# Two graph attention layers on one core: all stages of layer 0 before all of layer 1, adjacency loaded for every stage, one regular order

## The chip, the core and the metric

The kernel runs on one core of a Trainium2 chip. The metric is the device time of one execution in microseconds. The engines named here are PE (TensorE), DVE (VectorE), ACT (ScalarE), POOL (GpSimd) and SP (SyncE), which in this kernel only issues DMAs.

## The reference

Two layers act on x (8 batches, 1024 nodes, 128 features, float32) with a 0/1 adjacency adj (8, 1024, 1024, int32):

```
def _L0_gnn_ref(h, adj, W, a):
    Wh = jnp.einsum('bni,io->bno', h, W)
    e1 = Wh @ a1
    e2 = Wh @ a2
    e = e1[:, :, None] + e2[:, None, :]
    e = jnp.where(e > 0, e, ALPHA * e)
    scores = jnp.where(adj > 0, e, neg)
    attention = jax.nn.softmax(scores, axis=2)
    h_prime = jnp.einsum('bnm,bmo->bno', attention, Wh)
    return jax.nn.elu(h_prime)
...
h = jnp.maximum(_layernorm(x, axis=-1), 0.0)
x = x + _L0_gnn_ref(h, adj, L0_gnn_W, L0_gnn_a)
h = jnp.maximum(_layernorm(x, axis=-1), 0.0)
x = x + _L1_gnn_ref(h, adj, L1_gnn_W, L1_gnn_a)
```

Layer 1 is the same attention with other weights and without the elu. Both layers use the same adjacency of a batch.

## The kernel before, in words

The work is cut into 16 stages, one for each pair of layer and batch; `stages[n]` is that pair. The order before is layer 0 of batches 0, 1 and 2, then alternately layer 1 of batch b and layer 0 of batch b + 3, then layer 1 of batches 5, 6 and 7. The adjacency of a batch stays in one of three slots of `adj_sb` from its layer 0 to its layer 1, so each batch's adjacency (eight tiles of 128 x 1024) is loaded once.

The five engines have programs of their own, written out by hand, and meet through semaphores. In iteration n of its loop each engine finishes stage n - 1, runs stage n and prepares stages n + 1 and n + 2:

- PE: `project(n + 1)` makes W h of the next stage and the two attention terms from `hT`; `attend(n, t)` multiplies the masked weights of tile t (`pbuf`) into eight accumulators (`acc`); `spread_emax` and `turn_r` are single transposes; `transposes(n + 2)` turns the normalised x of a later stage. `spread_r` is eight transposes in the place of `turn_r`: it brings the row of exponentials to all partitions through PSUM.
- DVE: `masks(n, t)` makes `pbuf` from the row, a column and the adjacency tile; `take_acc(n - 1)` copies the three accumulator banks (`accs`) and takes the reciprocal; `copy_e` and `exp_args` prepare the exponentials of stage n + 1; `statistics` and `moments` are the layernorm statistics of a later stage; `add_elu` and `add_x` (after a layer 0 stage) or `add_hp` (after a layer 1 stage) update x.
- ACT: `scale_accs`, `exps`, `copy_r` (the row for the DMA) or `copy_row` (the spread row), `elu_exp`, `normalise`, `scale_wh`, `copy_hT`.
- POOL: the power for the layernorm.
- SP: all DMAs but four, in the order of its program. `load_row(m)` waits for `rT_ready`, writes the row to DRAM, waits for that, and reads it back broadcast to 128 partitions. An issue behind a wait in SP's program comes no earlier than that wait.

The DVE's masks of stage n + 1, t = 0, need `row_in` (or `row_copied`) and that PE is past the first tiles of stage n. PE's first product of stage n needs `acc_copied`, that is the copy of the accumulators of stage n - 1 by DVE. `before_drain(n)` is how many masks of stage n DVE makes before that copy.

Two stages (`LATE`, stages 3 and 15 here) need x of a stage only three places earlier, and the engines take other orders around them; stage n = 1 and stage n = AHEAD - 1 = 2 have orders of their own too. Stages in `SPREAD` (1 and 15) get their row by `spread_r`, the others by `load_row`. Stage n starts for PE where its `project(n + 1)` starts (in the regular order).

Of the kernel before, what the change touches and what calls it, by code (L numbers as in the profile page):

```python
# [5 lines left out]
P = 128  # L6
F32 = mybir.dt.float32
I32 = mybir.dt.int32
# [10 lines left out]
def gat_two_layers(nc, x, adj, w0, w0t, a0, w1, w1t, a1, r_rows, out):  # L19
# [7 lines left out]
    AHEAD = 3  # L27
    X_SLOTS = 6
# [15 lines left out]
    LATE = tuple(stage_of[1, b] for b in range(B) if stage_of[1, b] - stage_of[0, b] == 3)  # L44


    SPREAD = (1, LAST)
# [8 lines left out]
    with ExitStack() as ctx:  # L56
# [17 lines left out]
        adj_sb = sb("adj_sb", [P, AHEAD * T * N], I32)  # L74
        x_sb = sb("x_sb", [P, X_SLOTS * T * D])
# [40 lines left out]
        adj_in = [[sem(f"adj_in{s}_{t}") for t in range(T)] for s in range(AHEAD)]  # L116
# [60 lines left out]
        def x_at(b):  # L177
            s = (b % X_SLOTS) * T * D
            return x_sb[:, s:s + T * D]
# [4 lines left out]
        def adj_at(b, t):  # L184
            s = ((b % AHEAD) * T + t) * N
# [21 lines left out]
        def _(sp):  # L207
            def load_x(b):
                if b >= X_SLOTS:
                    sp.wait_ge(out_stored[b - X_SLOTS], 16)  # L210
                sp.dma_start(x_at(b), xv[b]).then_inc(x_in[b], 16)

            def load_adj(b, t):
                if b >= AHEAD:
                    sp.wait_ge(p_ready, T * stage_of[1, b - AHEAD] + t + 1)
                sp.dma_start(adj_at(b, t), adj[b, t]).then_inc(adj_in[b % AHEAD][t], 16)
# [29 lines left out]
            load_row(2)  # L246
            load_x(4)
            load_x(5)
            load_row(AHEAD)

            for n in range(AHEAD, LAST):
                l, b = stages[n]
                loads = l == 1 and b + AHEAD < B
                l_old, b_old = stages[n - 3]
                if l_old == 1 and b_old + X_SLOTS < B:
                    load_x(b_old + X_SLOTS)
# [77 lines left out]
        def _(act):  # L334
# [137 lines left out]
            for n in range(1, LAST + 1):  # L472
                elu = stages[n - 1][0] == 0
                if n == AHEAD - 1:

                    scale_accs(n - 1)
                    copy_hT(n + 1)
                    elu_exp(n - 1)
                    normalise(n + 2)
                    exps(n + 1)  # L480
                    copy_r(n + 1)
                    scale_wh(n + 1)
                    copy_hT(n + 2)
                    continue
                if n + 1 in LATE:
                    copy_hT(n + 1)
# [3 lines left out]
                if n + 2 in LATE:  # L490
                    elu_exp(n - 1)
                if n < LAST:
                    exps(n + 1)
                    if n + 1 in SPREAD:
                        copy_row(n + 1)
                    else:
                        copy_r(n + 1)
                    if n + 2 not in LATE:
                        elu_exp(n - 1) if elu else None
                    if n + 2 <= LAST and n + 2 not in LATE:  # L500
                        normalise(n + 2)
                    scale_wh(n + 1)
                if n + 2 in LATE:
                    normalise(n + 2)
                elif n + 2 <= LAST:
                    copy_hT(n + 2)

        @block.vector
        def _(dve):
# [145 lines left out]
            def masks(n, tiles):  # L655
                l, b = stages[n]
                for t in tiles:
                    if l == 0:
                        dve.wait_ge(adj_in[b % AHEAD][t], 16 * (b // AHEAD + 1))
                    if n == 0:  # L660
                        dve.wait_ge(row0_ready, 2)
                    elif t == 0:
# [3 lines left out]
                        else:  # L666
                            dve.wait_ge(row_in, 16 * loaded_rows(n))
                    nc.vector.scalar_tensor_tensor(pbuf[:, t, :], row_r[:, n % 2, :],  # L668
                                                   sqr[:, n % 2, 0, t:t + 1], adj_at(b, t),
# [83 lines left out]
            for n in range(1, LAST):  # L753
                l, b = stages[n - 1]
                if n + 2 <= LAST and not {n + 1, n + 2} & set(LATE):
                    statistics(n + 2)
                    moments(n + 2)
                masks(n, range(before_drain(n)))
                take_acc(n - 1)
                if n + 1 in LATE:  # L760
                    masks(n, (2, 3))
                    if n + 2 <= LAST:
                        statistics(n + 2)
                        moments(n + 2)
                    masks(n, (4,))
                    copy_e(n + 1)
                    masks(n, (5,))
                    exp_args(n + 1)
                elif n == 1:
                    copy_e(n + 1)  # L770
                    masks(n, (4,))
                    exp_args(n + 1)
                    masks(n, (5,))
                    add_elu(b)
                    add_x(b)
                    masks(n, (6,))
                    statistics(n + 2)
                    moments(n + 2)
                    masks(n, (7,))
                    continue  # L780
                elif n + 2 in LATE:
                    masks(n, (3,))
                    copy_e(n + 1)
                    masks(n, (4,))
                    exp_args(n + 1)
                    masks(n, (5,))
                    add_elu(b)
                    add_x(b)
                    statistics(n + 2)
                    moments(n + 2)  # L790
                    masks(n, (6, 7))
                    continue
                else:
                    if before_drain(n) == 1:
                        masks(n, (1,))
                    copy_e(n + 1)
                    masks(n, (2,))
                    exp_args(n + 1)
                    masks(n, (3, 4, 5))
# [16 lines left out]
        def _(pe):  # L816
# [176 lines left out]
            for n in range(1, LAST):  # L993
                if n + 1 in LATE:
                    k = 1 if n + 1 in SPREAD else 2
                    attend(n, range(k))
                    transposes(n + 1)
                    attend(n, (k,))
                    project(n + 1)
                    attend(n, (k + 1,))  # L1000
                    spread_emax(n + 1)
                    attend(n, (k + 2,))
                    spread_r(n + 1) if n + 1 in SPREAD else turn_r(n + 1)
                    attend(n, range(k + 3, 6))
                else:
                    project(n + 1)
                    attend(n, (0,))
                    spread_emax(n + 1)
                    attend(n, (1, 2) if n + 2 in LATE else (1,))
                    turn_r(n + 1)  # L1010
                    attend(n, (3, 4, 5) if n + 2 in LATE else (2, 3, 4, 5))
# [36 lines left out]
```

## Time and profile before

| what | value |
|---|---|
| time, median of 3 runs | 298.88 us (298.63 to 299.03) |
| the profiled execution: its own time | 298.75 us |
| its span in the trace | 296.9 us |
| PE, DVE, ACT, POOL busy | 290.6, 268.1, 167.3, 48.5 us |
| DMA moved | 49.50 MB, 167 GB/s mean |

The span runs from the first to the last instruction of the trace; the execution's own time has 1.85 us around it. Busy times are sums over one engine; matmul ends are modelled.

### The profile page before, as it was taken

To read this page: it belongs to the slowest core of one execution; us is meant where nothing else is said; L and a number is where in the kernel's file an instruction comes from. 1 tells how busy PE (TensorE), PEld (TensorE's weight loads), DVE (VectorE), ACT (ScalarE), POOL (GpSimd) and SP (SyncE) were. 2 spreads that over 40 slices of the span, in tenths; PEclk is the share of its full clock that TensorE was granted. 3 is DMA by queue.
4 is the path that set the end of the run, shared out by engine and by line. 5 is a ranking of instruction groups with operands and counts; after the bars stand their busy time and mean duration, and the time that the engine had idled before them with its cause. 6 is when DMAs were issued, how large, how long until landed. Compare 5 with 4: busy or idle time off the path is not lost.

```text
span 296.9 us, 6592 instructions
## 1 busy us (share of the span) xinstructions
PE 290.6 (98%) x2562; PEld 287.8 (97%) x2562; DVE 268.1 (90%) x613; ACT 167.3 (56%) x490; POOL 48.5 (16%) x53
## 2 busy tenths in 40 slices
PE   7999999999999999999999999999999999999996
PEld 7889999999999999999999999999999999999996
DVE  4796899889999989999899989999899989988796
ACT  3377482983856539382683737566393836384310
POOL 2712003205021120303003030210303000400000
PEclk9999999999999999999999999999999999999999
DMA  7999935004690347714584344903566110101012
GB/s 238 416 408 406 407 148 212 2 7 138 195 371 3 143 153 252 305 33 164 161 305 192 144 128 142 367 8 141 149 227 265 68 77 0 73 0 72 1 73 71
DMA packets 15215, 49.50 MB, mean 167 GB/s; under 512 B 2024, under 2 KB 3280, under 8 KB 15184
## 3 DMA queue, kind: packets, MB, share of 16 engines
q1 hardware_dynamic: 14608, 48.69, 44.4%
q8 instruction: 20, 0.33, 0.4%
q10 hardware_dynamic: 576, 0.39, 0.4%
q14 instruction: 11, 0.09, 0.1%
HBM read 44.83 MB, written 4.25 MB: 165 GB/s over the span
## 4 chain that ended last, share of the span: by engine, by line
PE 86%; DVE 7%; issue 2%; DMA 2%; ACT 2%; POOL 1%; DVEq 0%; POOLq 0%; ACTq 0%
PE acc L950 64%; PE prj L888 8%; PE tp L827 4%; DVE pbuf L668 3%; PE acc L965 2%; PE acc L819 2%; DMA row_r<-r_rows 1%; ACT xn L376 1%; DVE stats L563 1%; PE prj L891 1%; POOL rstd L281 1%; PE prj L860 1%; PE tp L910 1%; DVE accs L677 1%; PE prj L965 1%
## 5 line engine op out<-in xcount | busy, mean ns | idle before, releaser
L950 PE MATMUL acc<-wh,pbuf 128*128 128x129 f32 x1968 | 229.6, 275 | 0.9 <-DVE pbuf L644 0.3
L950 PEld LDWEIGHTS acc<-wh,pbuf 128*128 128x128 f32 x1968 | 225.1, 192 | 1.6 <-issue 0.9
L668 DVE SCALAR_TENSOR_TENSOR pbuf<-row_r,sqr,adj_sb 128x1024 f32<-128x1024 f32 x127 | 157.5, 1276 | 1.4 <-ACT row_r L416 1.0
L281 POOL TENSOR_TENSOR rstd<-vareps,neg_half 128x8 f32<-128x8 f32 x15 | 38.5, 2568 | 202.3 <-DVE vareps L581 202.2
L426 ACT ACTIVATE accs<-accs,rec 128x128 f32<-128x128 f32 x120 | 36.7, 389 | 51.0 <-DVE rec L687 51.0
L376 ACT ACTIVATE xn<-x_sb,shift,rstd 128x128 f32<-128x128 f32 x120 | 47.6, 478 | 0.0
L396 ACT ACTIVATE wh<-prj,wh 128x128 f32<-128x128 f32 x120 | 31.9, 357 | 0.0
L888 PE MATMUL prj<-w_ext,hT 128*128 128x130 f32 x240 | 29.3, 275 | 0.0
L888 PEld LDWEIGHTS prj<-w_ext,hT 128*128 128x128 f32 x240 | 28.0, 191 | 0.0
L382 ACT ACTIVATE hT<-tp 128x1024 f32<-128x1024 f32 x15 | 15.4, 1024 | 20.3 <-PE tp L827 20.3
L677 DVE TENSOR_TENSOR accs<-acc,uniform 128x387 f32<-128x387 f32 (+1 forms) x45 | 20.5, 506 | 2.9 <-PE acc L950 2.8
L563 DVE BATCH_NORM_STATS2 stats<-x_sb 128x6 f32<-128x128 f32 x112 | 22.9, 275 | 0.0
L827 PE MATMUL tp<-ident,xn 128*128 128x128 f32 x128 | 17.4, 277 | 0.3 <-DVE pbuf L668 0.3
L827 PEld LDWEIGHTS tp<-ident,xn 128*128 128x128 f32 x128 | 14.7, 142 | 1.0 <-DVE pbuf L668 0.4
L606 DVE COPY ecol<-prj 128x12 f32<-128x12 f32 x15 | 2.5, 167 | 10.8 <-PE prj L891 10.8
L373 ACT ACTIVATE act_gate<-shift 128x1 f32<-128x1 f32 x15 | 2.9, 192 | 14.1 <-POOL shift L284 14.1
L387 ACT ACTIVATE sqr<-args 128x24 f32<-128x24 f32 x15 | 3.3, 219 | 11.8 <-DVE args L640 11.8
L698 DVE TENSOR_TENSOR x_sb<-x_sb,ex 128x1024 f32<-128x1024 f32 x8 | 9.7, 1217 | 0.1
L692 DVE SCALAR_TENSOR_TENSOR ex<-accs,ex 128x1024 f32<-128x1024 f32 x8 | 9.7, 1218 | 0.0
L438 ACT ACTIVATE ex<-ex 128x1024 f32<-128x1024 f32 x8 | 8.5, 1058 | 0.3
L704 DVE TENSOR_TENSOR x_sb<-accs,x_sb 128x1024 f32<-128x1024 f32 x7 | 8.5, 1218 | 0.0
L436 ACT ACTIVATE ex<-accs 128x1024 f32<-128x1024 f32 x8 | 8.4, 1046 | 0.1
(105 smaller groups left out, 155.6 us busy)
## 6 DMA issues: line engine op xcount, KB each, us to landing
adj_sb<-in_adj SPq DMA_DIRECT2D x64, 512.0 KB, 6.5
row_r<-r_rows SPq DMA_DIRECT2D x13, 512.0 KB, 4.2
x_sb<-in_x SPq DMA_DIRECT2D x7, 512.0 KB, 6.4
out_x<-x_sb SPq DMA_DIRECT2D x7, 512.0 KB, 3.0
x_sb<-in_x ACTq DMA_DIRECT2D x1, 256.0 KB, 3.6
x_sb<-in_x SPq DMA_DIRECT2D x1, 256.0 KB, 3.4
r_rows<-rT SPq DMA_DIRECT2D x13, 4.0 KB
out_x<-x_sb SPq DMA_DIRECT2D x1, 192.0 KB, 1.9
```

Source lines behind the costliest of these rows:

```text
L281: nc.gpsimd.tensor_tensor(rstd[:, :], vareps[:, :], neg_half[:, :], ALU.pow).then_inc(rstd_ready, 1)
L376: nc.scalar.activation(xn[:, t, :], src[:, t, :], ACT.Identity, bias=shift[:, t:t + 1], scale=rstd[:, t:t + 1]).then_inc(xn_ready, 1)
L382: nc.scalar.activation(hT[:, :], tp[:, :], ACT.Relu, accum_out=hsum[:, :]).then_inc(hT_ready, 1)
L396: nc.scalar.activation(wh[:, m % 2, t, 0:D], prj[:, k, s * E:s * E + D], ACT.Copy, scale=wh[:, m % 2, t, D:C]).then_inc(wh_ready, 1)
L426: op = nc.scalar.activation(hp[:, t, :], hp[:, t, :], ACT.Copy, scale=rec[:, t:t + 1])
L563: st = nc.vector.bn_stats(stats[:, t, :], src[:, t, :])
L668: nc.vector.scalar_tensor_tensor(pbuf[:, t, :], row_r[:, n % 2, :], sqr[:, n % 2, 0, t:t + 1], adj_at(b, t), ALU.max, ALU.min).then_inc(p_ ...
L677: nc.vector.tensor_tensor(accs[:, k * NB:k * NB + w, :], acc[:, k, 0:w * C].rearrange("p (s c) -> p s c", c=C), uniform[:, e % 2, :].unsqu ...
L692: nc.vector.scalar_tensor_tensor(ex[:, :, :], hp, 0.0, ex[:, :, :], ALU.max, ALU.subtract).then_inc(hp_free, 1)
L827: return nc.tensor.transpose(tp[:, t * P:(t + 1) * P], xn[:, t, :], ident[:, :])
L888: nc.tensor.matmul(prj[:, k, s * E:(s + 1) * E], hT[:, t * P:(t + 1) * P], w_ext[:, l, :], start=(s == 0), stop=True, skip_group_check=True)
L950: mm = nc.tensor.matmul(sum_at(k, s), pbuf[:, t, i * P:(i + 1) * P], wh[:, n % 2, t, :], start=(t == 0 and s == 0 and k < NB), stop=(t == ...
```

## The change

The stages now run all of layer 0 (batches 0 to 7), then all of layer 1. The adjacency no longer stays for a second use: `load_adj(n, t)` takes a stage, not a batch, loads for every one of the 16 stages, and reuses slot n mod 3 when the masks of stage n - 3 have read the tile. `x_sb` holds all eight batches, so loading x waits for no store. Every distance between the layers of a batch is eight stages, and the orders of their own go: stages 1 to 14 follow one order on PE, DVE and ACT. Only stage 1 keeps `spread_r` and its four masks before the copy; stage 15 gets its row by `load_row`.

```
-    stages = [(0, b) for b in range(AHEAD)]
-    for b in range(B - AHEAD):
-        stages += [(1, b), (0, b + AHEAD)]
-    stages += [(1, b) for b in range(B - AHEAD, B)]
+    stages = [(l, b) for l in range(2) for b in range(B)]
...
-    SPREAD = (1, LAST)
+    SPREAD = (1,)
...
-            return {1: 4, AHEAD: 1, LAST - 2: 3}.get(n, 2)
+            return 4 if n == 1 else 2
...
             def load_x(b):
-                if b >= X_SLOTS:
-                    sp.wait_ge(out_stored[b - X_SLOTS], 16)
                 sp.dma_start(x_at(b), xv[b]).then_inc(x_in[b], 16)
...
+            def load_adj(n, t):
+                if n >= ADJ_SLOTS:
+                    sp.wait_ge(p_ready, T * (n - ADJ_SLOTS) + t + 1)
+                sp.dma_start(adj_at(n, t), adj[stages[n][1], t]).then_inc(adj_in[n % ADJ_SLOTS][t], 16)
...
-            load_row(2)
-            load_x(4)
-            load_x(5)
-            load_row(AHEAD)
...
+            for n in range(1, LAST):
+                loads = n + 2 <= LAST
                 if loads:
                     for t in range(3):
-                        load_adj(b + AHEAD, t)
-                if n + 1 not in SPREAD:
-                    load_row(n + 1)
+                        load_adj(n + 2, t)
+                load_row(n + 1)
+                if n + 3 < B:
+                    load_x(n + 3)
                 if loads:
                     for t in range(3, T):
-                        load_adj(b + AHEAD, t)
+                        load_adj(n + 2, t)
...
             for n in range(1, LAST):
                 l, b = stages[n - 1]
-                if n + 2 <= LAST and not {n + 1, n + 2} & set(LATE):
+                if n + 2 <= LAST:
                     statistics(n + 2)
                     moments(n + 2)
-                masks(n, range(before_drain(n)))
+                k = before_drain(n)
+                masks(n, range(k))
                 take_acc(n - 1)
...
-                elif n == 1:
-                    copy_e(n + 1)
-                    masks(n, (4,))
-                    exp_args(n + 1)
-                    masks(n, (5,))
-                    add_elu(b)
-                    add_x(b)
-                    masks(n, (6,))
-                    statistics(n + 2)
-                    moments(n + 2)
-                    masks(n, (7,))
-                    continue
...
+                copy_e(n + 1)
+                masks(n, (k,))
+                exp_args(n + 1)
+                masks(n, range(k + 1, 6))
...
             for n in range(1, LAST):
...
+                project(n + 1)
+                attend(n, (0,))
+                spread_emax(n + 1)
+                attend(n, (1,))
+                turn_r(n + 1)
+                attend(n, (2, 3, 4, 5))
+                if n + 2 <= LAST:
                     transposes(n + 2)
                 attend(n, (6, 7))
```

On DVE, from the last two masks of stage 0 to the copy of its accumulators, the kernel before runs (`pbuf` is a mask, `accs` an accumulator copy):

```order
L668 SCALAR_TENSOR_TENSOR pbuf<-row_r,sqr,adj_sb 128x1024 x6
L677 TENSOR_TENSOR accs<-acc,uniform 128x387 x2
L677 TENSOR_TENSOR accs<-acc,uniform 128x258
L687 RECIPROCAL rec<-accs 128x8
L606 COPY ecol<-prj 128x12
```

The changed kernel runs at the same place:

```order
L629 SCALAR_TENSOR_TENSOR pbuf<-row_r,sqr,adj_sb 128x1024 x2
L523 MEMSET gate 128x1
L526 BN_STATS stats<-x_sb 128x6 x8
L532 TENSOR_TENSOR mdiff<-stats 128x8
L534 SCALAR_TENSOR_TENSOR m2sum<-stats 128x8
L536 TENSOR_TENSOR mean<-stats 128x8
L539 SCALAR_TENSOR_TENSOR between<-mdiff 128x8
L541 TENSOR_SCALAR negmean<-mean 128x8
L544 SCALAR_TENSOR_TENSOR vareps<-m2sum,between 128x8
L629 SCALAR_TENSOR_TENSOR pbuf<-row_r,sqr,adj_sb 128x1024 x4
L638 TENSOR_TENSOR accs<-acc,uniform 128x387 x2
L638 TENSOR_TENSOR accs<-acc,uniform 128x258
```

The statistics and moments of stage 3 have moved in between the masks of stage 0 and those of stage 1.

On SP, from the end of the initial loads to the third row, the kernel before issues (`adj_sb<-in_adj` is an adjacency tile, `r_rows<-rT` and `row_r<-r_rows` the two halves of `load_row`):

```order
L216 DMA adj_sb<-in_adj 128x1024 x8
L221 DMA r_rows<-rT 8x128
L223 DMA row_r<-r_rows 128x1024
L211 DMA x_sb<-in_x 128x1024 x2
L221 DMA r_rows<-rT 8x128
L223 DMA row_r<-r_rows 128x1024
L216 DMA adj_sb<-in_adj 128x1024 x3
```

The changed kernel issues there:

```order
L207 DMA adj_sb<-in_adj 128x1024 x11
L212 DMA r_rows<-rT 8x128
L214 DMA row_r<-r_rows 128x1024
L202 DMA x_sb<-in_x 128x1024
L207 DMA adj_sb<-in_adj 128x1024 x8
L212 DMA r_rows<-rT 8x128
L214 DMA row_r<-r_rows 128x1024
L202 DMA x_sb<-in_x 128x1024
L207 DMA adj_sb<-in_adj 128x1024 x8
```

Three tiles of stage 3 now stand ahead of the first row, and one x and eight tiles between two rows.

On PE, in the last but one stage, the kernel before ends its preparation of stage 15 with:

```order
L896 MATMUL tp<-ident,emax 128x128
L950 MATMUL acc<-wh,pbuf 128x129 x8
L910 MATMUL tp<-ident,sqr 128x128 x8
L950 MATMUL acc<-wh,pbuf 128x129 x38
```

The changed kernel has there:

```order
L822 MATMUL tp<-ident,emax 128x128
L876 MATMUL acc<-wh,pbuf 128x129 x8
L844 MATMUL tp<-ident,sqr 8x128
L876 MATMUL acc<-wh,pbuf 128x129 x54
```

The eight transposes of `spread_r` have become the single one of `turn_r`.

## Rows read from the trace of the kernel before

**Rows 1.** The page: busy time, and 40 slices of 7.42 us each.

```profile
PE 290.6 (98%) x2562; PEld 287.8 (97%) x2562; DVE 268.1 (90%) x613; ACT 167.3 (56%) x490; POOL 48.5 (16%) x53
...
PEclk9999999999999999999999999999999999999999
...
GB/s 238 416 408 406 407 148 212 2 7 138 195 371 3 143 153 252 305 33 164 161 305 192 144 128 142 367 8 141 149 227 265 68 77 0 73 0 72 1 73 71
```

**Rows 2.** Windows by stage: busy time of each engine, clock, DMA share, GB/s.

```profile
34.79:51.52 16.73, 16.52 (x148) 16.33 (x148) 15.28 (x38) 8.76 (x26) 2.81 (x2) 1.00 0.54 217
51.52:88.49 36.97, 36.45 (x322) 35.88 (x323) 34.72 (x90) 25.61 (x71) 8.03 (x5) 1.00 0.39 139
88.49:105.89 17.40, 17.40 (x159) 17.38 (x158) 17.19 (x40) 9.45 (x30) 4.21 (x4) 1.00 0.23 82
105.89:123.29 17.40, 17.40 (x158) 17.38 (x158) 16.04 (x37) 11.48 (x32) 1.86 (x2) 1.00 0.76 268
```

**Rows 3.** The chain that ended last, in order of time: start, us, what.

```profile
36.80 1.79 PE acc L950 x16
...
42.27 0.12 PE tp L918
...
42.71 1.21 DMA r_rows<-rT
43.94 4.35 DMA row_r<-r_rows
...
271.81 0.87 PE tp L910 x8
```

**Rows 4.** Timeline of DVE, 12 to 90 us: start, us, what, idle before.

```profile
29.68 4.87 DVE L668 SCALAR_TENSOR_TENSOR pbuf<-row_r,sqr,adj_sb 128x1024 f32<-128x1024 f32 x4 [1.03 <-ACT row_r L416]
34.47 1.35 DVE L677 TENSOR_TENSOR accs<-acc,uniform 128x387 f32<-128x387 f32 x3
...
48.42 2.48 DVE L668 SCALAR_TENSOR_TENSOR pbuf<-row_r,sqr,adj_sb 128x1024 f32<-128x1024 f32 x2 [0.37 <-DMA row_r<-r_rows]
50.83 1.35 DVE L677 TENSOR_TENSOR accs<-acc,uniform 128x387 f32<-128x387 f32 x3
...
73.69 0.16 DVE L606 COPY ecol<-prj 128x12 f32<-128x12 f32 x1
```

**Rows 5.** Timeline of SP's queue: the load of x of batch 3.

```profile
15.04 1.07 SPq L211 DMA_DIRECT2D x_sb<-in_x  x1
```

**Rows 6.** DMA issues in 15.0 to 15.1 us: KB, us to landing.

```profile
x_sb<-in_x SPq DMA_DIRECT2D x1, 512.0 KB, 15.9
```

**Rows 7.** Timeline of DVE, 88 to 124 us.

```profile
89.32 1.35 DVE L677 TENSOR_TENSOR accs<-acc,uniform 128x387 f32<-128x387 f32 x3
...
90.83 0.12 DVE L606 COPY ecol<-prj 128x12 f32<-128x12 f32 x1
...
107.94 0.17 DVE L606 COPY ecol<-prj 128x12 f32<-128x12 f32 x1 [1.08 <-PE prj L891]
...
114.23 1.22 DVE L692 SCALAR_TENSOR_TENSOR ex<-accs,ex 128x1024 f32<-128x1024 f32 x1
...
118.90 0.29 DVE L563 BATCH_NORM_STATS2 stats<-x_sb 128x6 f32<-128x128 f32 x1
...
123.74 0.55 DVE L677 TENSOR_TENSOR accs<-acc,uniform 128x387 f32<-128x387 f32 x1
```

**Rows 8.** Timeline of ACT, 105 to 124 us.

```profile
110.77 0.22 ACT L387 ACTIVATE sqr<-args 128x24 f32<-128x24 f32 x1 [1.43 <-DVE args L640]
...
112.97 1.06 ACT L438 ACTIVATE ex<-ex 128x1024 f32<-128x1024 f32 x1
```

**Rows 9.** DMA issues near 44.3, 119.4 and 148.7 us: KB, us to landing.

```profile
x_sb<-in_x SPq DMA_DIRECT2D x1, 512.0 KB, 5.2
...
x_sb<-in_x SPq DMA_DIRECT2D x1, 512.0 KB, 7.3
...
adj_sb<-in_adj SPq DMA_DIRECT2D x1, 512.0 KB, 5.4
```

More of the change, by code:

```diff
@@ L26, in gat_two_layers @@
     HALF = T // 2
-    AHEAD = 3
-    X_SLOTS = 6
+    ADJ_SLOTS = 3
     LAST = 2 * B - 1
@@ L115, in gat_two_layers @@
         x_in = [sem(f"x_in{b}") for b in range(B)]
-        adj_in = [[sem(f"adj_in{s}_{t}") for t in range(T)] for s in range(AHEAD)]
+        adj_in = [[sem(f"adj_in{s}_{t}") for t in range(T)] for s in range(ADJ_SLOTS)]
         out_stored = [sem(f"out_stored{b}") for b in range(B)]
@@ L489, in _ @@
                 scale_accs(n - 1)
-                if n + 2 in LATE:
-                    elu_exp(n - 1)
                 if n < LAST:
                     exps(n + 1)
[L494 to L500, printed above, removed]
+                    copy_r(n + 1)
+                    elu_exp(n - 1) if elu else None
+                    if n + 2 <= LAST:
                         normalise(n + 2)
                     scale_wh(n + 1)
-                if n + 2 in LATE:
-                    normalise(n + 2)
-                elif n + 2 <= LAST:
+                if n + 2 <= LAST:
                     copy_hT(n + 2)
@@ L655, in masks @@
             def masks(n, tiles):
-                l, b = stages[n]
                 for t in tiles:
-                    if l == 0:
-                        dve.wait_ge(adj_in[b % AHEAD][t], 16 * (b // AHEAD + 1))
+                    dve.wait_ge(adj_in[n % ADJ_SLOTS][t], 16 * (n // ADJ_SLOTS + 1))
                     if n == 0:
@@ L754, in _ @@
                 l, b = stages[n - 1]
-                if n + 2 <= LAST and not {n + 1, n + 2} & set(LATE):
+                if n + 2 <= LAST:
                     statistics(n + 2)
                     moments(n + 2)
-                masks(n, range(before_drain(n)))
+                k = before_drain(n)
+                masks(n, range(k))
                 take_acc(n - 1)
-                if n + 1 in LATE:
-                    masks(n, (2, 3))
-                    if n + 2 <= LAST:
-                        statistics(n + 2)
-                        moments(n + 2)
-                    masks(n, (4,))
-                    copy_e(n + 1)
-                    masks(n, (5,))
-                    exp_args(n + 1)
-                elif n == 1:
[L770 to L773, printed above, removed]
-                    add_elu(b)
-                    add_x(b)
-                    masks(n, (6,))
-                    statistics(n + 2)
-                    moments(n + 2)
-                    masks(n, (7,))
[L780 to L799, printed above, removed]
+                copy_e(n + 1)
+                masks(n, (k,))
+                exp_args(n + 1)
+                masks(n, range(k + 1, 6))
                 if l == 0:
@@ L993, in _ @@
             for n in range(1, LAST):
[L994 to L1011, printed above, removed]
-                if n + 2 <= LAST and n + 2 not in LATE:
+                project(n + 1)
[4 more added lines that the diff above has]
+                attend(n, (2, 3, 4, 5))
+                if n + 2 <= LAST:
                     transposes(n + 2)
```

34 lines of the change are left out of this document (6 added, 28 removed).

## The prediction, made before the changed kernel was run

> **What bounds the kernel now.** I read the page first, then the windows by stage, then the chain that ended last, and only then the single engines around the first four stages. The page [rows 1] says PE 98% busy, with the granted clock at its upper level (2.4 GHz) in all 40 slices. The windows [rows 2] say where the missing 2% lies. A regular stage (project, eight attend tiles, two small transposes, eight transposes of a later stage) takes exactly 17.40 us, with PE busy for 17.40 of them, whether the DMA share is 0.76 or 0.23. So from 88.49 us on, the kernel is PE's own work, and nothing gained on DVE, ACT or DMA is worth anything there; DMA traffic doesn't slow PE either. Before that, stage 1 takes 16.73 us although it holds no transposes (17.40 less the 0.87 of eight transposes [rows 3], so 16.53), and stages 2 and 3 take 36.97 us where their content is 2 x 17.40 + 0.87 = 35.67. The whole slack outside start and tail is thus 0.20 + 1.30 = 1.50 us.
>
> **The change, part by part.** The sum is made against the profiled execution: span 296.9 us, its own time 298.75, that is 0.13 below the median of 298.88.
>
> 1. The last stage's row. PE's eight spreading transposes (0.87 us in the chain) become one transpose (0.12, as in the other stages) [rows 3]. PE is the bound there, so -0.75. The row now comes by DMA: turn to write 0.44, write to broadcast 1.23, landing 4.35, together 6.02 us after a transpose at 5.7 us into stage 14, so it lands near 11.7; the masks of stage 15 were reached no earlier than that in a regular stage (from the statistics' end at 13.0 + 2.4 us on), and PE asks for them only at its stage end, 16.5. Hidden.
>
> 2. The irregular orders of stages 1 to 3 go. If the regular order runs there as it does later, all 1.50 us of slack come back: -1.50.
>
> 3. A wait is put in the place of them. The regular order puts the statistics of stage n+2 ahead of the masks of stage n, in n = 1 too. There they are those of batch 3, and SP still loads batch 3's x behind sixteen adjacency tiles. It is issued at 15.04 [rows 5] and lands 15.9 later [rows 6], at 30.94. In the kernel before, DVE ends the masks of stage 0 at 28.65, idles 1.03 for the row and starts stage 1's masks at 29.68 [rows 4]; x of batch 3 is asked for only after all of these. Now DVE waits for it: start at 31.07 (a mask started 0.13 after its row landed, 43.94 + 4.35 = 48.29 against 48.42 [rows 3, 4]), statistics 2.44 (118.90 to 123.74 is 4.84, less two masks of 1.20 [rows 7]), four masks 4.79 (29.68 to 34.47), so the accumulators are copied from 38.30 instead of 34.47. Behind the waiting statistics on DVE stand the masks of stage 1 and this copy, and for the copy waits PE: its first product of the next stage came 0.69 after a copy began (50.83 [rows 4]; the window boundary 51.52 [rows 2] is that product). So PE goes on at 38.99, where it was ready at 36.80 [rows 3]: +2.19. Nothing hides it: PE has no other work between, since the transposes of stage 3 stand later.
>
> 4. What is late next. Stage 2 begins at 34.79 + 17.40 + 2.19 = 54.38. On DVE: copy_e 1.51 after the copies begin (89.32 to 90.83 [rows 7]), at 39.81; the exponentials start 2.83 and end 3.05 after copy_e (107.94 [rows 7]; 110.77 + 0.22 [rows 8]), at 42.9 at most, and PE reaches its transpose at 38.99 + 1.79 + 0.12 + 1.79 = 42.7. The row write is issued 0.44 later, at 43.2 to 43.3. Three more adjacency tiles now lie in the queue ahead of it: SP's run of tiles without a row has eleven instead of eight, as the order shows. The initial loads fill the queue at 408 GB/s until about 39.7 (slice six, from 37.1, holds 148 GB/s [rows 1]); three tiles of 0.524 MB add 3.9 us, to 43.6, and their landing about 45.0. The write lands between 44.5 (no hindrance, 1.23) and 45.0. x of batch 4 is now issued right behind the row, 0.39 later (43.94 to 44.33), and lands 5.2 to 5.4 after its issue: 5.2 is x in this very place, 5.4 an adjacency tile of the same size in this place with more tiles behind [rows 9]. So x lands at 50.1 to 50.8. DVE arrives there at about 50.2: it also waits for ACT's elu, done 3.26 after the exponentials start (110.77 to 112.97 + 1.06 [rows 8], 0.5 of it a wait that is shorter here), so at 42.64 + 2.8 to 3.3, near 45.5; from the add of the elu to the statistics it is 4.67 (114.23 to 118.90 [rows 7]). Copies for stage 1 then begin at 55.1 to 55.8, 0.7 to 1.4 into stage 2, where a regular stage has 0.45. PE needs the first bank at 2.01 - 0.69 = 1.32, and its row transpose has 0.59 to spare. That is 0 to 0.4 us of stall; I take 0.15, nearer the lower end, because DVE's uninterrupted cycle (73.69 to 90.83, 17.14 us, with all of the elu work in it [rows 4, 7]) regains 0.26 per stage.
>
> 5. The regular loop with x in it. x of stages 4 to 7 is now fetched one stage ahead, right behind the row, where before it had stages of room. This makes a closed loop: copy_e to exponentials 3.05, turn to write 0.44, write to row issue 1.23, to x issue 0.39, landing 5.4, 0.13, statistics and two masks 4.84, copies to copy_e 1.51: 16.99 us, against PE's 17.40. It costs nothing as long as x lands within 5.8 us of its issue. Bounds: 0 at 5.4; for 7.3 see the rivals.
> The Trainium skill speaks against this place: "DMA: Bandwidth & Descriptors", section "Latency and other measured facts", gives HBM's latency as 0.2 us on average and 2 us at high load. By an estimate from that page, 1.8 us more would put the landing at 7.2 and the loop at 18.8. The trace doesn't bear it out at this spot: the same landing is 5.2 in an idle queue and 5.4 with four tiles following.
>
> 6. Twice the adjacency traffic: 8 x 0.524 + x 0.524 + row 0.524 = 5.2 MB, 12.8 us at 408 GB/s of each 17.40. Issued from 7.3 us into a stage, it is through 4.3 us into the next, before the next row write at 6.1. Cost 0; it was already so in the stage with share 0.76 [rows 2]. The cover is 1.8 us; gone, it would feed the loop of point 5. Larger x storage drops SP's waits for stores: no one waited there, 0.
>
> Sum: -0.75 - 1.50 + 2.19 + 0.15 = +0.09. Span 297.0, time 298.84 for the profiled run, 298.97 beside the median: I say **299.0**. A difference under 0.2%, 0.6 us, is about what a measurement of this kernel can't tell from none. Own range of this case: stall of point 4 from 0 to 0.9 and landing of x of batch 3 within half a microsecond: 298.3 to 300.2.
>
> **The rivals.**
> A, slower: the x loop of point 5 binds. Decides at a landing of 5.8 us. For it: a late x took 7.3 [rows 9], though behind five adjacency tiles, and the loop has only 0.41 us. Against: in its new place it has none ahead. At 6.4, midway between these ends, the loop is 17.99, 0.59 too long, four times, less the 0.59 in hand: +1.8, 300.8. At 7.3: 4 x 1.49 - 0.59 = +5.4, 304.4. Chance 0.17.
> B, faster: the wait for batch 3 isn't paid, as x lands by 29 or PE's order absorbs it. Then 2.19 and 0.15 fall away: 296.7. Against: the landing row [rows 6], and SP's order up to there, which the change leaves alone. Chance 0.10.
> C, slower: DVE becomes the bound in the eight stages in a row that carry elu work; before, a lighter one followed each. 17.14 against 17.40 says no, but only 0.26 is left. If hand-overs between engines make it 17.7, eight stages cost 0.3 each: 301.4. Chance 0.08.
> D, slower: the 2.2 us gap lowers PE's clock to 1.2 GHz. The 1.50 us of gaps in stages 1 to 3, spread over three stages, did not [rows 1, 2]. If a fifth of stage 1's remaining 15.4 us ran at half speed, +3.1: 302. Chance 0.04.
> The Trainium skill, "TensorE: Matmul & The Clock Gate", section "HAM oscillation", says that idle gaps let the gate fall back; no gap of this trace is long enough to show it.
> Something unlisted: 0.03.
>
> **How the numbers follow.** My case has 0.58, so 299.0 is the prediction. Outside 297.6 to 302.0 lie B (0.10), the dear half of A (0.08) and little else. Faster by over 0.2%: B and 0.09 of my case, 0.19. Within: 0.41. Slower: A, C, D, the rest of my case and the unlisted, 0.40.
>
> **What would show it.** Step 3: DVE idle about 2.4 us before the first statistics of stage 1's iteration, released by DMA x, and PE idle near 2.2 us at 36.8, released by the accumulator copy. Step 1: stage 14 of 16.53 us, no spreading transposes. Step 2: stages 2 and 3 of 17.40 each with a little on top. Step 5: x landing 5.2 to 5.8 after its issue, and DVE no later into stages 3 to 6 than 1.1 us at its copies. I am wrong if stages 2 to 6 exceed 17.6, if the clock shows under 1.0 after 39 us, or if PE doesn't wait at 36.8.

## The result and the profile after

| | before | changed |
|---|---|---|
| median of 12 executions | 298.88 us | 301.7 us |
| lowest | 298.50 us | 298.85 us |
| the profiled execution, its own time | 298.75 us | 299.89 us |
| its span | 296.9 us | 298.1 us |
| DMA moved | 49.50 MB | 83.59 MB |

The ratio of changed to before is 1.0063, 95% interval 1.004 to 1.0086: slower by 0.6%. It is close to the ratio of the means (301.04 to 299.21 us); the medians alone are 0.9% apart, because the changed kernel's median falls into the dearer of two groups. These groups differ in the granted clock: four executions at 1.00 took 298.85 to 299.99 us, seven at 0.994 or 0.989 took 301.26 to 302.52 us. The twelfth, 374.26 us at a clock of 0.85, was disturbed and is left out of what follows. The profiled execution belongs to the first group.

The page of the changed kernel, to be held against [rows 1] (busy time, 40 slices of 7.45 us, DMA traffic):

```profile
PE 289.7 (97%) x2555; PEld 287.2 (96%) x2555; DVE 268.2 (90%) x613; ACT 166.4 (56%) x489; POOL 47.8 (16%) x53
...
PE   7999969999999999999999999999999999999996
...
GB/s 230 417 405 409 407 353 226 403 200 411 191 365 329 247 411 153 412 125 308 327 247 385 112 411 138 346 342 220 374 214 401 209 320 382 208 291 118 25 73 70
```

PE has one hole, in the sixth slice, where before it had none. The windows by stage of the changed kernel (boundaries near those of its stages, columns as in [rows 2]: PE busy, PE weight loads, DVE, ACT, POOL, granted clock, DMA share, GB/s):

```profile
34.79:54.30 19.51, 16.78 (x151) 16.62 (x150) 16.49 (x39) 11.47 (x32) 3.08 (x2) 1.00 0.83 314
54.30:71.70 17.40, 17.34 (x156) 17.18 (x155) 17.20 (x40) 11.47 (x32) 3.02 (x3) 1.00 0.81 320
71.70:89.10 17.40, 17.40 (x158) 17.38 (x158) 17.08 (x39) 11.47 (x32) 2.95 (x3) 1.00 0.75 299
```

The first row lacks 2.7 us of PE, the second next to nothing, the third is full: DVE has 17.1 us of work in each 17.40 and PE doesn't wait for it, at twice the adjacency traffic. The two timelines around the hole, DVE's and PE's, answer to [rows 4] and [rows 3]:

```profile
26.35 2.48 DVE L629 SCALAR_TENSOR_TENSOR pbuf<-row_r,sqr,adj_sb 128x1024 f32<-128x1024 f32 x2
31.77 0.29 DVE L526 BATCH_NORM_STATS2 stats<-x_sb 128x6 f32<-128x128 f32 x1 [2.94 <-issue]
...
34.22 4.87 DVE L629 SCALAR_TENSOR_TENSOR pbuf<-row_r,sqr,adj_sb 128x1024 f32<-128x1024 f32 x4
39.01 1.35 DVE L638 TENSOR_TENSOR accs<-acc,uniform 128x387 f32<-128x387 f32 x3
```

```profile
36.59 0.39 PE L817 MATMUL prj<-w_ext,hsum 128*128 128x128 f32 x2
39.71 2.02 PE L876 MATMUL acc<-wh,pbuf 128*128 128x129 f32 x16 [2.73 <-DVE accs L638]
```

And the load of x of batch 3, in the timeline of SP's queue and with its time to landing:

```profile
15.15 1.07 SPq L202 DMA_DIRECT2D x_sb<-in_x  x1
```

```profile
x_sb<-in_x SPq DMA_DIRECT2D x1, 512.0 KB, 16.6
```

15.15 + 16.6 = 31.75, and DVE starts its statistics at 31.77. The view puts that wait down as "issue", since it names no DMA there; the landing time names it. PE waits 2.73 us for the accumulator copy at the end of that queue of work. In this execution the clock stays at 1.00 throughout; no execution of the changed kernel with a low clock was profiled.

### The profile page after: what moved, and what is told of

The parts are those of the page before. It is cut to its first block, busy times and chain, and to the rows that moved or that the text cites. A ratio compares the mean times of both kernels' runs of the same rounds, so it can differ in the third digit from the quotient of the medians.

```text
span 298.1 us, 6643 instructions
## 1 busy us (share of the span) xinstructions
PE 289.7 (97%) x2555; PEld 287.2 (96%) x2555; DVE 268.2 (90%) x613; ACT 166.4 (56%) x489; POOL 47.8 (16%) x53
## 2 busy tenths in 40 slices
DMA packets 24591, 83.59 MB, mean 280 GB/s; under 512 B 3072, under 2 KB 4336, under 8 KB 24560
## 4 chain that ended last, share of the span: by engine, by line
PE 92%; DVE 5%; issue 2%; POOL 0%; ACT 0%; POOLq 0%; DVEq 0%
PE acc L876 70%; PE prj L814 8%; PE tp L753 5%; DVE pbuf L629 3%; PE acc L891 2%; PE acc L745 2%; PE prj L817 1%; PE prj L786 1%; PE tp L822 1%; PE prj L891 1%; PE prj L876 1%; PE acc L795 1%; PE tp L844 1%; DVE stats L526 0%; PE tp L828 0%
## 5 line engine op out<-in xcount | busy, mean ns | idle before, releaser
L405 ACT ACTIVATE rT<-tp 8x128 f32<-8x128 f32 x14 | 3.7, 267 | 6.2 <-PE tp L844 6.2
```

## The experiments

Each ratio is to executions of the kernel before that ran beside the run. "Low clock" counts the executions with a granted clock under 0.998. Of the 69 undisturbed executions of the kernel before beside these runs, one had a low clock (304.82 us at 0.989). Twelve of the 28 beside e1 to e4 took 299.87 to 300.59 us with the clock at 1.00, about 1.5 us more than the others; why stays open, and those four ratios hold that spread.

| run | median us | ratio to before (95%) | low clock | PE gap in the profiled execution |
|---|---|---|---|---|
| changed kernel | 301.7 | 1.0063 (1.004 to 1.0086) | 7 of 11 | 2.73 at 37 us |
| e1_x3_early | 299.84 | 1.0015 (0.999 to 1.0041) | 5 of 12 | 2.91 at 54, 0.41 at 75 us |
| e2_gap_filled | 299.67 | 1.0012 (0.9995 to 1.0029) | 0 of 12 | filled |
| e3_gap_in_before | 303.45 | 1.0152 (1.0119 to 1.0185) | 5 of 6 | 2.17 at 37, 0.49 at 55 us |
| e4_traffic_in_before | 299.18 | 0.9993 (0.9973 to 1.0012) | 0 of 12 | as before |
| e5_x3_x4_early | 297.89 | 0.9967 (0.9949 to 0.9984) | 0 of 12 | 0.63 at 54, 1.66 at 72 us |
| e6_x3_x4_row2_early | 297.66 | 0.9962 (0.9939 to 0.9985) | 1 of 12 | 1.06 at 72 us |
| e7_last_row_only | 303.67 | 1.0155 (1.0126 to 1.0184) | 6 of 6 | 3.64 at 279 us |
| e8_after_again | 300.62 | 1.0054 (1.0026 to 1.0082) | 6 of 12 | 2.12 at 37, 0.18 at 74 us |
| e9_x_one_stage_ahead | 296.77 | 0.9934 (0.9908 to 0.9959) | 0 of 6 | none |
| e10_row15_spread | 297.24 | 0.9943 (0.9923 to 0.9962) | 0 of 6 | none |
| e11_x_behind_tiles | 334.96 | 1.1205 (1.1155 to 1.1255) | 6 of 6 | 2.76, 6.86, 6.76, 5.84, 6.88 |

### Is it the wait for x of batch 3? (e1)

```
+            load_x(3)
             for t in range(T):
                 load_adj(1, t)
-            load_x(3)
```

> The changed kernel with one line moved: x of batch 3 is loaded ahead of stage 1's adjacency tiles instead of behind them. Theory (the wait for x of batch 3 on DVE holds PE up, and the gap in PE is what lowers the granted clock in some executions): DVE starts stage 3's statistics near 28.9 us without a wait, PE's gap at 36.8 falls from 2.7 us to under 0.3, the span falls by 2.7 to 2.9 us to 295.2 to 295.5, the time to about 297.1, and the granted clock stays 1.00 in every execution, so the spread of the times closes to under 0.5 us. Rival (the constant adjacency traffic, 280 GB/s, is behind the slower executions): the span still falls by 2.7 us at best, but executions with a clock of 0.994 and 2 to 3 us more go on appearing in about half of the runs.

The hole at 37 us went, as both theories said, but the time hardly fell, as neither did. Five of twelve executions still had a low clock, as the rival said; whether the new hole or the traffic is behind them, this run can't tell. PE's and DVE's timelines of this kernel show it one stage later:

```profile
53.60 0.39 PE L817 MATMUL prj<-w_ext,hsum 128*128 128x128 f32 x2
56.90 2.02 PE L876 MATMUL acc<-wh,pbuf 128*128 128x129 f32 x16 [2.91 <-DVE accs L638]
```

```profile
51.35 0.29 DVE L526 BATCH_NORM_STATS2 stats<-x_sb 128x6 f32<-128x128 f32 x1 [3.85 <-issue]
```

This wait is for x of batch 4. The SP queue of this kernel shows why:

```profile
40.71 0.34 SPq L212 DMA_DIRECT2D r_rows<-rT  x1
45.33 0.35 SPq L214 DMA_DIRECT2D row_r<-r_rows  x1
45.72 0.43 SPq L202 DMA_DIRECT2D x_sb<-in_x  x1
```

The row's write of 4 KB, 1.2 us in an empty queue [rows 3], took 4.6, because the eleven tiles issued before it were still running: the DMA share is 1.02 up to 43 us, 0.58 in 43 to 44 and 0.19 in 44 to 45. The row and x came behind it. In the changed kernel the shares of 43 to 45 us are the same (0.57, 0.18), but its write is issued only at 44.07. So x of batch 4 lands at nearly the same time in both, 51.3 here (45.72 + 5.6) and 51.8 there (46.37 + 5.4): the backlog of the initial loads sets it, and a PE that is 2.7 us earlier waits for it that much longer. My expectation missed this.

### Traffic or gap: what lowers the clock? (e2, e3, e4, e8)

e2 fills PE's gap with work that computes nothing, and leaves the wait:

```
                 project(n + 1)
+                if n == 1:
+                    for _ in range(24):
+                        nc.tensor.transpose(tp[:, 0:P], ident[:, :], ident[:, :])
                 attend(n, (0,))
```

> The changed kernel with 24 transposes of the identity into the idle transpose tile, placed where PE waits for the accumulator copy (about 2.6 us of PE work that computes nothing). The wait for x stays. Theory (gap lowers the clock): the time of an execution with the clock at 1.00 is unchanged, about 299.1 to 299.9, give or take 0.3, but no execution shows a clock under 0.998, and the median falls from 301.7 to about 299.5. Rival (traffic, or the kernel's power, lowers the clock): executions at 0.994 and 301 to 302.5 us remain as frequent.

No execution of 12 had a low clock, and the median fell to 299.67. The traffic is that of the changed kernel.

e3 puts the gap alone into the kernel before; the extra statistics go to a scratch tile and change no result:

```
+                if n == 1:
+                    dve.wait_ge(x_in[3], 16)
+                    for t in range(12):
+                        nc.vector.bn_stats(scratch[:, t, :], x3_at(3)[:, t % T, :])
                 masks(n, range(before_drain(n)))
```

> The kernel before with the stall alone: ahead of stage 1's masks DVE waits for x of batch 3 and does twelve statistics of 128x128 into a scratch tile (2.45 us, the length of the changed kernel's statistics and moments). Traffic and order stay as before. Theory: DVE starts at about 31.1, PE gets a gap of 2.0 to 2.9 us at 36.8, the time rises by 2 to 3 us, and if the gap lowers the clock some executions show 0.994 and 2 to 3 us more on top. Rival (traffic): the gap costs its own length and no execution shows a lower clock than the kernel before does.

Its profiled execution is one with a low clock. PE's timeline and the windows (PE busy, PE weight loads, DVE, ACT, POOL, granted clock, DMA share, GB/s):

```profile
38.94 3.12 PE L955 MATMUL acc<-wh,pbuf 128*128 128x129 f32 x16 [2.17 <-DVE accs L678]
41.85 0.42 PE L901 MATMUL tp<-ident,emax 128*128 128x128 f32 x1
42.07 4.22 PE L955 MATMUL acc<-wh,pbuf 128*128 128x129 f32 x32
```

```profile
36.00:39.00 3.00, 0.83 (x8) 0.67 (x7) 3.00 (x4) 0.00 (x0) 0.00 (x0) 1.00 1.03 414
39.00:42.00 3.00, 3.00 (x17) 3.00 (x18) 2.46 (x8) 2.13 (x8) 0.00 (x0) 0.61 0.24 96
42.00:45.00 3.00, 3.00 (x24) 3.00 (x23) 2.53 (x7) 2.76 (x6) 0.00 (x0) 0.82 0.00 0
45.00:48.00 3.00, 3.00 (x29) 2.98 (x28) 2.96 (x3) 1.57 (x7) 0.00 (x0) 1.00 0.03 7
```

The clock is at its upper level while PE idles, falls once PE works again, and is back before 45 us. In windows of half a microsecond it is 1.00 up to 39.5, 0.50 (the lower level, 1.2 GHz) in each from 40 to 43, and 1.00 again from 43.5. In 39 to 45 us PE is busy throughout and gets through 41 matmul records (17 + 24), where 6 us at 1.00 hold 58 (two such windows as the last, of 29). The dear parts are the first tile, 3.12 us instead of 2.02, and the next two, 4.22 instead of 3.74. With the 0.15 of the small transpose that is 1.7 us. At this moment the DMA share was 0.24 and then 0. So a gap alone does it, without the added traffic. The span is 4.4 us above that of the kernel before (301.3 to 296.9). The gap of 2.17, a second one of 0.49 at 55.3 us behind a late row, and the clock's 1.7 make 4.36. The one execution of six with the clock at 1.00 took 303.49 us, so in this kernel the clock's price is not visible between executions. Something besides the clock differs between them, perhaps the gaps; that wasn't looked at.

e4 puts the traffic alone into the kernel before: the adjacency is loaded for each stage, in the old order of stages. Its core:

```
-            def load_adj(b, t):
-                if b >= AHEAD:
-                    sp.wait_ge(p_ready, T * stage_of[1, b - AHEAD] + t + 1)
-                sp.dma_start(adj_at(b, t), adj[b, t]).then_inc(adj_in[b % AHEAD][t], 16)
+            def load_adj(n, t):
+                if n >= AHEAD:
+                    sp.wait_ge(p_ready, T * (n - AHEAD) + t + 1)
+                sp.dma_start(adj_at(n, t), adj[stages[n][1], t]).then_inc(adj_in[n % AHEAD][t], 16)
```

> The kernel before in its own stage order, with its adjacency loaded for every stage (twice the traffic, slots by stage). Theory: traffic is hidden, the time is within 0.3 us of the kernel before, 298.9, with a clock of 1.00. Rival (traffic slows PE or lowers the clock): 1 to 3 us more, or executions with 0.994 in about half of the runs.

299.18 us, ratio 0.9993, clock 1.00 in all 12. A window over eight stages of it shows PE filling all of its time under a DMA share of 0.76:

```profile
123.29:263.00 139.71, 139.71 (x1253) 139.37 (x1252) 132.96 (x291) 82.51 (x246) 21.75 (x16) 1.00 0.76 291
```

e8 repeats the changed kernel as it is.

> The changed kernel once more, on the chip and between the runs of this call. Theory: two groups of times again, about 299 to 300 us with the clock at 1.00 and 301 to 302.5 us with 0.994, the second in about half of the executions. Rival (the groups belong to the chip of the first runs): one group only.

Six executions at 1.00 took 298.8 to 300.03 us; six at 0.988 to 0.994 took 301.21 to 304.17. The groups belong to the kernel. The profiled execution, one at 1.00, has x of batch 3 landed earlier than the first time (statistics from 31.21 instead of 31.77) and a gap of 2.12 instead of 2.73 us: the gap's length varies between executions. Together these four runs show that the gap lowers the clock and the traffic doesn't: filled, it goes (0 of 12); put in alone, it comes (5 of 6); the traffic alone does nothing (0 of 12).

### Removing the gaps (e5, e6, e9)

e5 also loads x of batch 4 early, ahead of stage 2's tiles.

> The changed kernel with x of batch 3 loaded ahead of stage 1's adjacency tiles and x of batch 4 ahead of stage 2's (it stood behind row 2). Theory (with x of batch 3 early the same gap only moved: DVE then waited 3.85 us for x of batch 4, which stood behind row 2 and its eleven tiles, and PE got its 2.9 us gap at 54 us): both gaps go; what stays is row 2 itself, issued near 46.6 and landing near 50.9, about when DVE wants it, so at most 0.3 us of gap at 54. Span 295.0 to 295.4, time about 297.0, clock 1.00 in every execution. Rival (a fixed backlog: whatever loads first, some transfer is late by 2.5 us around 50 us): the gap at 54 stays at 2 us or more and the time stays above 298.5.

```
+            load_x(3)
             for t in range(T):
                 load_adj(1, t)
-            load_x(3)
+            load_x(4)
...
-                if n + 3 < B:
+                if n > 1 and n + 3 < B:
                     load_x(n + 3)
```

The first kernel faster than before. But 0.63 us of gap stay at 54 (DVE waits 1.59 for row 2), and 1.66 at 72 us (DVE waits 2.12 for x of batch 5). The profiled execution is the slowest of the twelve (299.05 us), so the typical gaps may be smaller. My figure of 297.0 was 0.9 low, again for the backlog one stage further on; its rival had it half right.

e6 issues row 2 ahead of stage 3's tiles as well:

```
-                if loads:
+                if loads and n > 1:
                     for t in range(3):
                         load_adj(n + 2, t)
                 load_row(n + 1)
+                if n == 1:
+                    for t in range(3):
+                        load_adj(n + 2, t)
```

> As the one before, and in iteration 1 SP issues row 2 ahead of the three tiles of stage 3 instead of behind them. Theory: row 2 lands near 46.5, DVE waits for nothing in stages 1 and 2, PE has no gap over 0.1 us from 35 us on; span 294.9, time 296.7, clock 1.00 in every execution: 2.2 us under the kernel before (0.75 of the last row, 1.50 of the slack). Rival (DVE is too slow for eight elu stages in a row): a gap in PE appears in stages 3 to 8 and eats the gain.

The gap at 54 is gone, the one at 72 stays at 1.06. The SP queue of this kernel tells where x of batch 5 loses its time: the write of row 3 takes over 3 us.

```profile
58.12 0.29 SPq L212 DMA_DIRECT2D r_rows<-rT  x1
61.36 0.33 SPq L214 DMA_DIRECT2D row_r<-r_rows  x1
61.73 0.43 SPq L202 DMA_DIRECT2D x_sb<-in_x  x1
```

Nothing waits for DVE in stages 4 to 8, so the rival (DVE too slow for eight such stages) is out.

e9 keeps what e6 has (x of batches 3 and 4 and row 2 early) and gives every later x a stage more too: behind row n + 1 comes x of batch n + 4. The line that differs, against the changed kernel:

```
-                if n + 3 < B:
-                    load_x(n + 3)
+                if n + 4 < B:
+                    load_x(n + 4)
```

> The changed kernel with every x loaded one stage earlier: x of batches 3 and 4 ahead of stage 1's and stage 2's tiles, x of batch n + 4 behind row n + 1, and row 2 ahead of stage 3's tiles. Theory (what is left of the loss after the last experiment is one more x behind a row whose write stands in the backlog of tiles: DVE waited 1.84 us for x of batch 5 and PE 1.06 us at 72): that gap goes too; row 3 lands near 66.8, just before DVE wants it near 67.5. No PE gap over 0.3 us after 30 us, span 294.6 to 294.9, time 296.4 to 296.8 in every execution with the clock at 1.00; the spread of 3 us between executions, which comes from landing times, shrinks to under 1 us. Rival (the backlog moves the wait on to row 3): DVE waits 1 us or more for row 3 near 67.5, and PE has about 0.5 to 1 us at 72.

Windows of stages 1 and 2 of this kernel, and the count from its page:

```profile
34.60:52.00 17.40, 17.40 (x158) 17.38 (x158) 15.33 (x37) 11.47 (x32) 2.09 (x1) 1.00 0.86 332
52.00:69.40 17.40, 17.40 (x158) 17.38 (x158) 16.97 (x39) 11.47 (x32) 2.70 (x3) 1.00 0.84 316
```

```profile
PE 288.7 (98%) x2555; PEld 286.8 (97%) x2555; DVE 268.4 (91%) x613; ACT 166.4 (57%) x489; POOL 47.8 (16%) x53
```

No wait of PE is left after 30 us in this trace; the span is 294.3 us. The traced execution is the fastest of six; they take 296.15 to 298.10 us, a spread of 2 us and not under 1 as I had said, and the slower ones weren't seen. By its median this kernel is the fastest of all: 0.9934 of the kernel before.

### The last row (e7, e10)

e7 takes the first term of the sum into the kernel before: `SPREAD = (1,)` instead of `(1, LAST)`, nothing else.

> The kernel before with one part of the change alone: stage 15 gets its row by the DMA instead of eight transposes on PE. Theory: PE is the bound there, so 0.75 us less, 298.1 against 298.9. Rival (the row's 6 us round trip is late for stage 15's masks, or PE has slack there): no gain, within 0.2 us.

It is slower by 1.55%. PE's timeline at the end of stage 14, and DVE's:

```profile
273.41 0.27 PE L918 MATMUL tp<-ident,sqr 128*8 128x128 f32 x1
273.52 5.52 PE L950 MATMUL acc<-wh,pbuf 128*128 128x129 f32 x48
282.68 2.92 PE L950 MATMUL acc<-wh,pbuf 128*128 128x129 f32 x12 [3.64 <-DVE accs L677]
```

```profile
279.58 2.48 DVE L668 SCALAR_TENSOR_TENSOR pbuf<-row_r,sqr,adj_sb 128x1024 f32<-128x1024 f32 x2 [3.34 <-DMA row_r<-r_rows]
```

In the old order of stage 14 (it is a `LATE` neighbour) the row's transpose comes 5.5 us before PE is through with its last tile of the stage (273.41 to 278.9). The row's round trip alone is 6.0, and two masks and the start of the copy stand behind it. The clock falls as well, in all six executions: in the trace it is 1.00 in 280 to 281 us, while PE idles, and 0.51 in 281 to 282, still before PE goes on. PE's next 28 matmuls take 5.69 us (282.68 to 288.37), where 28 of the last stage in the changed kernel take 3.13 (282.55 to 285.68): a loss of 2.6. The gap of 3.64 and these 2.6, less the 0.75 saved, make the 5.5 us by which the span grew (302.4 to 296.9). The DMA share was 0.05 in 280 to 281 us and 0.00 behind that.

The regular order has the row's transpose near the start of the stage (266.81 in e10, below), with the whole of that stage's PE work behind it. So this is not a clean test of the term: it shows that the DMA row is only free together with the regular order. The clean test is e10, the kernel of e9 with the spread row back in stage 15:

```
-                turn_r(n + 1)
+                spread_r(n + 1) if n + 1 in SPREAD else turn_r(n + 1)
```

> The kernel of the run before with stage 15's row spread by eight transposes on PE again, in the regular order. It measures the first term of the prediction's sum by itself. Theory: PE is the bound in stage 14, so +0.75 us against the run before. Rival (the round trip of the row costs something there as well): no difference or less time.

The medians differ by 0.47 us (297.24 to 296.77), less than the spread between executions, so the times neither confirm the 0.75 nor speak against it. The trace gives the term itself; PE's timeline of e10 in stage 14:

```profile
266.81 1.04 PE L844 MATMUL tp<-ident,sqr 128*128 128x128 f32 x8
267.68 12.22 PE L884 MATMUL acc<-wh,pbuf 128*128 128x129 f32 x108
```

0.87 us from the one start to the other, without a wait around, against 0.11 for the single transpose.

### The closed loop with x in it (e11)

```
-                if n + 3 < B:
-                    load_x(n + 3)
                 if loads:
                     for t in range(3, T):
                         load_adj(n + 2, t)
+                if n + 3 < B:
+                    load_x(n + 3)
```

> The changed kernel with x of batches 4 to 7 issued behind the iteration's tiles instead of right behind the row: issued about 3.1 us after the row and landing about 7.3 us later, 10.4 after the row instead of 5.8. Theory (the closed loop row, x, statistics, copy, exponentials of 16.99 us with x at 5.4): the loop becomes 21.6 us, PE has a gap of about 4 us in each of stages 2 to 5, together 15 to 17 us, and each gap is long enough to bring the clock down for about 3 us, 1.6 us more each: 320 to 326 us in all. Rival (the waits for x overlap with other slack): less than 8 us more.

335 us, dearer than I said. PE's timeline of one turn:

```profile
63.94 3.78 PE L876 MATMUL acc<-wh,pbuf 128*128 128x129 f32 x16 [6.86 <-DVE accs L638]
67.52 0.42 PE L822 MATMUL tp<-ident,emax 128*128 128x128 f32 x1
...
90.41 3.78 PE L876 MATMUL acc<-wh,pbuf 128*128 128x129 f32 x16 [6.76 <-DVE accs L638]
```

The loop's own terms can be put in for each turn. In the first, from PE's start at 39.45 to 63.94, x was issued 4.95 us after the row (45.03 to 49.98) and landed 8.4 later, 13.35 behind the row where the sum of 16.99 has 5.79. That makes 24.55; the turn took 24.49. The gap at its start, 2.76 us, had left the clock at 1.00.

The second turn, the one shown, took 26.5. Here the row's write took 2.29 instead of 1.23, and x was issued 3.05 after the row and landed 9.1 later, 12.15 behind it: 24.4. The first tile of this turn takes 3.78 us instead of 2.02 and the transpose behind it 0.15 more, at the lowered clock and inside the loop: together 26.3. So the loop's arithmetic holds when the measured landings are put in, and a gap that lowers the clock makes the next one longer.

The clock falls within these gaps: PE idles from 57.1 to 63.9 us, and the clock is 1.00 up to 61 and 0.50 from 61.5. My expectation was low because x landed 8.4 to 9.3 us after its issue, where I had 7.3.

## Why the prediction came out as it did

The time lay within the stated range of 297.6 to 302.0, near its upper end, on the side "slower", to which I had given 0.40. It lay outside the range of my own case, which ended at 300.2. That the wide range held it is in part luck: most of the chance that I had put on its upper part was that of A and C (300.8 and 301.4), and what carried the time there was D. Of the three signs of being wrong that I had named, one came (a clock under 1.0, in 7 of 11 executions, though its place in time wasn't seen), one came barely (stage 2 took 17.69 us, over 17.6) and one didn't (PE does wait at 36.8). By its steps:

**Step 1, the last row, -0.75.** Held in the traces: 0.87 against 0.11 us of PE. What step 1 said about the hiding row holds in the regular order only (e7).

**Step 2, the slack of stages 1 to 3, -1.50.** Held: stage 3 and all after it take 17.40, and with x on time stages 1 and 2 do as well (e9).

**Step 3, the wait for x of batch 3, +2.19.** The mechanism was right to the instruction, place and releaser. The size was 2.96: in the chain of work that ended last, stage 1 takes 20.36 us from its first matmul to that of stage 2 (34.97 to 55.33), against 17.40. Most of the difference is x, which landed at 31.75 instead of 30.94, so that PE went on at 39.71 instead of 38.99 (+0.72). The 36.80 from which I counted is the chain's time; PE's own timeline of the kernel before starts that tile at 36.63 (+0.17), and stage 1 now begins about as much later (-0.19). The first tile behind a gap also takes 1.86 us to the next start (39.71 to 41.57) instead of 1.79 (+0.07), which the sum had left out.

**Step 4, what is late next, +0.15.** Measured 0.29 (55.33 to 73.02 is 17.69), of which 0.23 is PE's later start behind the accumulator copy (57.40 instead of 57.17) and the rest the first tile behind it. DVE waited for x of batch 4 0.99 us, where I had 0 to 0.6.

**Step 5, the loop.** x of batches 4 to 7 landed 5.4, 5.1, 5.5 and 5.2 us after issue, where I had 5.2 to 5.4 and a limit of 5.8. The loop is real (e11), and in the changed kernel it didn't bind. The Trainium skill's sentence on HBM latency under load ("DMA: Bandwidth & Descriptors", "Latency and other measured facts") would, by my estimate from it, have made it 7.2; the trace doesn't agree for this transfer. The DMA engines were nearly idle when it was issued, though (share 0.03 in 45 to 46 us, 0.17 in 46 to 47).

**Step 6, twice the traffic, 0.** Held in the stages (e4). The cover before the next row write was smaller than I said: of the tiles issued from 81.22 us on, the last bytes moved between 95.5 and 96 (DMA share 0.21), over 5 us into the stage that began at 90.26, where I had 4.3; the next write came at 96.55. (My 4.3 doesn't follow from my own 7.3 and 12.8 either, which give 2.7.) What it hid from me is the small write: behind a full queue it takes 3 to 5 us instead of 1.2 (e1, e6, e9), and the 1.9 of the changed kernel fits with the time that its queue had gained by the hole at 37 us.

**The sum.** For an execution with the clock at 1.00 I had a span of 297.0; it was 298.1: 0.19 from a later start of stage 1, 0.77 from step 3, 0.14 from step 4. Those four executions took 298.85 to 299.99, by their mean 0.5 us more than the 299.0 that I had said.

**What failed is the chance of rival D**, not its mechanism. I gave 0.04 to "the 2.2 us gap lowers PE's clock", on the ground that 1.50 us of gaps in three stages hadn't. It happened in 7 of 11 executions, and in 6 of 12 when repeated. The low-clock group is 2.5 us dearer by its mean in the first (301.95 to 299.46) and 3.1 in the second (302.55 to 299.43), where I had priced it at 3.1 by a fifth of a stage that no row showed. Not all of that need be the clock: by e3's trace the clock costs 1.7 us behind a gap of this size, and the executions with a low clock may have had the longer gaps. None of them was profiled in this kernel. The gaps of the kernel before, none over 0.36 us in these stages, were no evidence about one of 2 to 3. That step decides the median: with the gap filled (e2) it is 299.67. The Trainium skill ("TensorE: Matmul & The Clock Gate", "HAM oscillation") says that idle gaps let the gate fall back; e3's windows agree, with 0.61 after a gap of 2.17 us. The Trainium skill's rule in that section is for longer gaps than this one, and here the measurement decides.

**Where the gain went.** The change had 2.25 us to give. The wait for x took it all back and 1 us more (2.96 and 0.29), and the fall of the clock came on top. With x a stage earlier (e9) the gain is there: 2.1 us by the medians (298.83 to 296.77), close to the sum of steps 1 and 2.

Open: why the clock falls in some executions and not in others. A longer gap there is not ruled out, but length alone doesn't decide: the clock fell behind 2.17 us in e3 and stayed at 1.00 behind 2.76 in e11. One execution of e6, whose profiled gap is 1.06 us, also had 0.989 at 303.13 us; its own gap wasn't seen.

## What to carry to other kernels

When work is moved earlier in a fixed order, look up for each of its inputs when it is asked for now, and trace that transfer's issue: a load that was free for having 13 us of room (landed at 30.9 us, first read at 44.4) becomes a wait of 3 us without being touched. A late queue isn't cured by moving one transfer up, since the lateness shows at the next one; count the queue's bytes against the clock until it has caught up, small writes with a wait behind them included. And where PE is the bound, price a gap twice: its length, and the chance that the clock falls after it, which here split one kernel's times into two groups 2.5 to 3 us apart.

## What the runs showed of the hardware that I had not expected

- The granted clock can fall after PE has gone back to work: 1.00 over 36 to 39 us with PE mostly idle, 0.61 over 39 to 42 with PE busy (e3). Behind longer gaps it fell while PE was still idle (e7, e11). Either way the lower level outlasted PE's return: the loss was 1.7 us behind a gap of 2.17 (e3), 2.6 behind 3.64 (e7), and 2.1, 2.5, 1.5 and 2.1 behind gaps of 6.86, 6.76, 5.84 and 6.88 (e11). It shows no steady growth with the gap.
- How often it fell went with the traced gap: in 0 of 12 executions with the gap filled (e2), 0 of 12 and 1 of 12 where the gaps are 1.66 us at most (e5, e6), about half at 2.1 to 2.9 us (the changed kernel, e1, e8), 5 of 6 in e3, all six at 3.64 us and more (e7, e11).
- A DMA of 4 KB took 1.2 us in an empty queue, 1.9 behind the tail of a backlog and 4.6 behind all of it (e1), 5.0 in e9 (58.02 to 63.00).
- A DVE busy for 17.1 to 17.2 of each 17.40 us, in stages 2 to 8 running, never held PE up once x was on time (stages 3 to 8 of the changed kernel, PE busy for all of each 17.40).
